# Second stage of a linear-attention and feed-forward kernel: VectorE's norms behind the quotients, ScalarE's copy of the transform's columns behind the upper part

## The reference

```python
qf, kf = elu(rope(x @ Wq.T)) + 1, elu(rope(x @ Wk.T)) + 1
num, den = causal_sums(qf, kf, v)            # per head and token
out = num / (den + 1e-6)
x = layernorm(x + out @ Wo.T)
h = fwht(x * SU_ug) / 64
h = silu(h @ W_gate.T * s_gate) * (h @ W_up.T * s_up)
h = fwht(h * SU_dp) / 64
x = layernorm(x + h @ W_down.T * s_down)
```

## Time and profile before

| | |
|---|---|
| time of the runs | 2311.16 us median of 3 (2309.01 to 2311.57) |
| span of the profiled execution | 2310.1 us (core 0, the only one); no time of its own is given beside it, so what lies around it is taken from the median of the runs, 1.1 us above |
| TensorE busy | 2254.4 us, 98% of the span |
| VectorE busy | 1825.1 us, 79% |
| ScalarE busy | 1273.1 us, 55% |
| GpSimd busy | 1129.0 us, 49% |
| DMA | 252.75 MB, 109 GB/s over the span |
| granted TensorE clock, mean | 0.994 |

### The profile page before, as it was taken

How to read it: one execution, slowest core, us unless ns; L and a number is a source line. 1 busy time by engine, 2 the same in 40 slices (tenths; PEclk the granted TensorE clock), 3 DMA queues, 4 the chain that set the end, 5 groups by cost and what they waited for, 6 DMA issues and landing times.

```text
span 2310.1 us, 32819 instructions
## 1 busy us (share of the span) xinstructions
PE 2254.4 (98%) x10209; PEld 1823.0 (79%) x10209; DVE 1825.1 (79%) x2452; ACT 1273.1 (55%) x2285; POOL 1129.0 (49%) x1002
## 2 busy tenths in 40 slices
PE   7999999999999999999999989999999999999998
PEld 5778787787878786787777768888888888888887
DVE  7877777778686868787887896787888788878877
ACT  6666666666676767233334455454545554455443
POOL 4667676767676767455544733321242133303321
PEclk9999999999999999999999999999999999999999
DMA  4110101111120215777767541323233323222323
GB/s 153 37 65 37 68 34 66 47 58 62 39 73 28 73 60 192 255 246 254 245 229 261 187 140 62 123 78 113 79 101 92 118 81 98 92 82 83 98 67 101
DMA packets 132701, 252.75 MB, mean 109 GB/s; under 512 B 44576, under 2 KB 45344, under 8 KB 122880
## 3 DMA queue, kind: packets, MB, share of 16 engines
q1 hardware_dynamic: 132608, 251.60, 32.5%
HBM read 188.11 MB, written 63.44 MB: 109 GB/s over the span
## 4 chain that ended last, share of the span: by engine, by line
PE 71%; issue 11%; POOL 9%; DVE 5%; ACT 2%; DMA 1%; SPq 0%; POOLq 0%; ACTq 0%; DVEq 0%
PE pj L548 17%; PE pj L629 11%; PE pnum L629 6%; PE pj L643 5%; PE psc L629 5%; PE pj L558 4%; PE pst L629 4%; PE psc L643 4%; PE pnum L643 3%; PE psc L579 3%; PE pnum L597 3%; PE pnum L600 3%; PE pst L643 2%; POOL fa L1338 2%; PE pst L586 1%
## 5 line engine op out<-in xcount | busy, mean ns | idle before, releaser
L1368 POOL TENSOR_TENSOR wcs<-wcr 128x256 f32<-128x256 f32 x64 | 67.7, 1058 | 515.3 <-DVE wcl L1107 504.3
L1401 POOL TENSOR_TENSOR tb<-tb,sinb 128x512 f32<-128x512 f32 x160 | 224.0, 1400 | 91.7 <-ACT tb L928 90.9
L548 PE MATMUL pj<-xah,wqh 128*128 128x512 f32 x512 | 204.3, 399 | 4.3 <-DVE Kf L1243 3.0
L1404 POOL TENSOR_TENSOR Ql<-tb,Qh 128x512 fp32r<-128x512 f32 x128 | 169.7, 1328 | 70.2 <-ACT Qh L937 70.1
L478 PE MATMUL pj<-woh,oh 128*128 128x512 f32 x512 | 202.9, 396 | 0.0
L548 PE MATMUL pj<-xal,wqh 128*128 128x512 f32 x512 | 200.5, 392 | 0.0
L548 PE MATMUL pj<-xah,wql 128*128 128x512 f32 x512 | 200.5, 392 | 0.0
L478 PE MATMUL pj<-woh,ol 128*128 128x512 f32 x512 | 200.4, 391 | 0.0
L478 PE MATMUL pj<-wol,oh 128*128 128x512 f32 x512 | 200.3, 391 | 0.0
L1231 DVE TENSOR_TENSOR pj<-pj,cosb 128x512 f32<-128x512 f32 x160 | 111.1, 694 | 69.7 <-ACT tb L928 69.6
L629 PE MATMUL pj<-xch,wch 128*128 128x512 f32 x384 | 150.9, 393 | 7.9 <-DVE xcl L1113 4.7
(11 more groups left out here) (258 smaller groups left out, 7070.8 us busy)
## 6 DMA issues: line engine op xcount, KB each, us to landing
num_scratch<-no SPq DMA_DIRECT2D x128, 256.0 KB, 2.4
nt<-num_scratch SPq DMA_DIRECT2D x32, 1024.0 KB, 5.5
rb<-rden_scratch SPq DMA_DIRECT2D x32, 1024.0 KB, 6.3
wdr<-wd_scratch SPq DMA_DIRECT2D x128, 256.0 KB, 3.3
wcr<-in_wg SPq DMA_DIRECT2D x64, 256.0 KB, 2.8
wcr<-in_wu SPq DMA_DIRECT2D x64, 256.0 KB, 3.1
xst<-in_xT SPq DMA_DIRECT2D x34, 256.0 KB, 3.8
xr<-in_x SPq DMA_DIRECT2D x32, 256.0 KB, 5.6
```

What stands on the lines that cost most here:

```text
L548: last = nc.tensor.matmul(bank[:, :], w[:, b, :], x[:, b, :], start=(k == 0), stop=(k == 11))
L1401: nc.gpsimd.tensor_tensor(tb[c][:, :], tb[c][:, :], sinb[:, :], ALU.mult).then_inc(sin_done, 1)
L1404: nc.gpsimd.tensor_tensor(Ql[g % 2][:, c, :], (tb[c] if c else Kf)[:, :], f32(Qh[g % 2][:, c, :]), ALU.subtract).then_inc(lo_done, 1)
```

## The change

On VectorE the quotient of block n+2 is put in front of the norm of block n-1, directly behind the lower part of block n+1; the order of a step becomes sums, lower, divide, norm, then columns_lo in j = 3. On ScalarE the copy `split(m-1)`, which rounds the transform's columns, leaves the end of step j = 2 and comes behind `upper` in step j = 3 of the same group. Nothing is added or removed, and no wait changes.

```diff
@@ ScalarE, step(m, j, at)
                 if at + 1 < NC:
                     upper(1 - s, n + 1, at + 1)
+                if j == 3 and at >= NCH:
+                    split(m - 1)
                 if at == 1:
@@
                 if j == 2 and at >= NCH:
                     fold_out(m - 1)
-                    split(m - 1)
                 if j == 3 and at >= NCH:
                     evict(m - 1)
@@ VectorE, step(m, j, at)
                 if at + 1 < NC:
                     lower(1 - s, n + 1)
+                if at + 2 < NC:
+                    divide(s, n + 2, m * 2 + j // 2 + 1)
                 if at >= 1:
                     norm(1 - s, n - 1)
                 if j == 3 and at >= NCH:
                     columns_lo(m - 1)
-                if at + 2 < NC:
-                    divide(s, n + 2, m * 2 + j // 2 + 1)
```

## The result

The changed kernel takes 2321.71 us (median of 5, 2319.49 to 2324.13), the kernel before 2311.16 us (median of 5): 10.6 us more, ratio 1.0048 with an interval of 1.0036 to 1.0060. It is slower, on the side that was forecast, and inside the full range of 2318 to 2338; it lies 0.3 us under the 2322 to 2332 of the forecast's own case, and the point, 2327.6, was 5.9 us too high.

A forecast was written before the change was run, and what follows sets the result against it. TensorE's matmuls bound the stage (busy 404.66 of 420 us), so only its waits count. Groups 14.1 plus opening 2.3 give 16.4 us; on the 2310.1 span, plus 1.1, 2327.6 us; range 2322 to 2332, with rivals 2318 to 2338.

The forecast's parts named there:

- the forecast's own case: Whole kernel: the worked-out sum of later norms holds, 2327.6 us, within 2322 to 2332; chance 0.71.
- j = 0, +1.86: First step of a group: quotient and GpSimd's scaling go before the norm, so TensorE's transposes start 1.86 us late.
- j = 1, +0.43: Second step of a group: quotient delays GpSimd's root, an addition precedes the norm; transposes wait 1.02 us, before 0.59.
- j = 2, -0.51: Third step of a group: the transposes no longer wait for the norm, where they waited 0.51 us before.
- j = 3, +0.27: Fourth step of a group: upper part goes before the copy, quotient before the norm; wait 0.4 us for 0.14.
- Opening, +2.3: Step 2 of the stage: a 2.3 us quotient lies before an already late norm, +2.3 us, bounds 0 to 4.
- The last group, +1.8: Last of seven groups: no quotient in j = 2 and 3, so it loses 1.8 us.
- Six groups, +12.3: The six groups before the last: each has the whole group sum of +2.05 us, +12.3 in all.
- A: VectorE's norm goes ahead of a waiting GpSimd instruction, saving 1.1 us in j = 0; 2320 us, chance 0.10.
- B: TensorE's granted clock falls in each of seven groups, 8.7 us on top; 2336 us, chance 0.10.
- C: Quotient fills VectorE's 2.94 us hole in j = 1 for nothing; -1.24 us a group, 2303 us, chance 0.04.
- D: Losses in j = 0 and gains in the rest cancel, added wait under 0.6 us; 2311 us, chance 0.05.

## Why the prediction was right, and where its sum was off

The forecast was slower by 16.4 us with 0.71 for its own case (2322 to 2332); it was slower by 10.6, 0.3 us under the foot of that case. The path that the forecast names is the one that the runs show; three of its terms were mis-sized, all of them too high. Its steps one by one:

- **j = 0, +1.86: measured +1.40.** The order quotient, scaling, norm is as worked out, and the scaling's turn was 0.96 us. The failed step is "the root waited during it and takes its turn of 0.3 to 0.4". The quotient at 1085.98 takes 2.28 us with the root still running to 1086.47 beside it: the root, one element a row, takes nothing from VectorE. That is 0.46 us a group, 2.8 in six groups; the other steps give 0.15 a group of it back.
- **j = 1, +0.43: measured +0.45.** Both causes, a root pushed back and an addition ahead of the norm, are in the rows. With the additions short the wait is 0, so all of it hangs on the additions; the two causes were not taken apart.
- **j = 2, -0.51: measured -0.51.**
- **j = 3, +0.27: measured +0.40.** The copy costs nothing where it stands; kept in front it would cost 1.8, and did (2.32 against 0.54).
- **Opening, +2.3: measured about 0** (974.47 - 974.95 = -0.5 at the transposes of step 3; the profiled execution of after comes to the stage's first matmul 0.8 us earlier). The failed step is "a quotient of 2.3 us now lies before that norm: +2.3". The quotient does lie there, but most of it falls into the 4.26 us for which VectorE waited for the root before, so the norm is 1.1 us later (962.45 for 961.31) and not 2.3. The first transposes waited 2.2 us, the second 1.3 instead of 3.2. Beside that, the kernel before loses clock behind its 3.05 us wait, and needs 13.04 us from these transposes to the next, where the changed kernel needs 11.43. In the changed kernel the clock fell one step earlier, where the loss lies in front of the next wait, and not there:

```profile
948.00:952.00 4.00, 3.28 (x12) 0.70 0.19 70
960.00:964.00 4.00, 2.83 (x16) 1.00 1.02 422
964.00:968.00 4.00, 4.00 (x19) 1.00 1.07 286
```

VectorE's rows there show also what the prediction priced too low: the quotient waits for its operands. The first row is the kernel before, the others are the changed one.

```profile
961.31 0.55 DVE L1005 TENSOR_SCALAR x<-x,mv,rstd 128x512 f32<-128x512 f32 x1 [4.26 <-POOL rstd L1321]
```

```profile
944.17 3.09 DVE L1034 TENSOR_TENSOR nt<-nt,rb 128x2048 f32<-128x2048 f32 x1 [1.97 <-DMA nt<-num_scratch]
...
960.24 2.29 DVE L1034 TENSOR_TENSOR nt<-nt,rb 128x2048 f32<-128x2048 f32 x1 [2.77 <-DMA rb<-rden_scratch]
```

- **The last group, +1.8: measured -1.2** (from the transposes of j = 3 before it, 1281.71 and 1271.83, to the last ones of the stage). The failed step is "the last has no quotient in j = 2 and 3 and loses 1.8": it takes j = 2 as in every group and says nothing of j = 3 and of the stage's end. Measured were waits of +1.28, +0.55, -0.88 and -0.51, and 1.6 us less where TensorE passes to the next stage.
- **Six groups, +12.3: measured +10.4** (307.24 for 296.88 us, from 974.47 and 974.95 to the same two places).

Opening, six groups and last group are too high by 2.8, 1.9 and 3.0 us; together that is 7.7, from the forecast's 16.4 to the 8.7 of the profiled pair. That the total still came out inside the range is owed to the six groups; opening and last group, forecast as losses, were none.

From the groups the profiled pair gives 2.6 + 5 x 1.74 - 2.5 = 8.8 us, against 8.7 read at the last transposes and 7.7 in the span; the medians differ by 10.6. The difference of up to 3 us between the pair and the medians lies within the 3.6 and 4.6 us by which runs of one kernel differ.

The rivals: A (the norm goes ahead of a waiting GpSimd instruction) did not happen, the norm of j = 0 takes 1.49 to 1.51 us in all seven groups. B (the clock, once a group) did not happen, the new waits being 1.4 us; it came at 2.2 us in the opening, where it cost nothing that shows, and at 2.3 us in groups of the kernel with the quotient alone. C (the hole is free) was tried by itself in the one step that has a hole and fell. D (losses and gains cancel) fell with the waits of 1.40 and 1.04 us.

Where the Trainium skill was weighed, the rows decided: the norm contends with GpSimd, 1.50 us against 0.54 in the changed kernel too. That does not go against the rule, which leaves out the two-port modes, and the norm's operation is on the section's list of those that can enter one; whether it does here no run shows. The same section's rule that the first to be issued keeps the port for its whole instruction ("SBUF — State Buffer", who interferes with whom) fits the rows shown here with GpSimd instructions of 512 elements; the root of j = 0, which ran to its end beside a quotient of undisturbed length (2.28 us), does not show the blocking that the rule has.

## What to carry to other kernels

An engine's idle time in front of a wait is not free room if the work put there holds something that the awaited engine needs. Here VectorE's hole was the time in which GpSimd's additions ran, and a quotient in it pushed the root, and so the norm, back (a wait of 2.6 us for 0.6); ask of each hole what the other engine does in it. Where a short instruction that many wait for stands in a queue behind long ones that nobody waits for yet, move the long ones (two additions moved by a step brought 8 us, from 4.0 to 12.2 under before) before touching the engine that waits. And put an instruction with a waiting consumer ahead of one whose consumer has slack: the quotient is needed a step later, the norm at once.

## What the runs showed that was not expected

- A GpSimd instruction on one element a row did not hold up VectorE's next instruction (the quotient behind the root, 2.28 us in j = 0 and in j = 2), while one on 512 elements does, by 0.96 to 1.1 us.
- The length of TensorE's wait alone does not say whether the granted clock falls from 2.4 to 1.2 GHz. With the quotient alone it fell at four of six waits of 2.3 us, and at none of the two in the opening, 2.2 and 3.2 us; with the quotient first in j = 1 at two of six of 2.6 us and not at 2.2 us in the opening, where the changed kernel's fell. No wait of the transposes of 1.8 us or less brought it down in any of the runs. A fall lengthened the group by 1.1 us (54.66 - 53.52) with the quotient alone and by 1.3 (52.20 - 50.86) with the quotient first in j = 1. Two stretches of TensorE of the kernel with the quotient first in j = 1, each around a wait of 2.6 us, the first with a fall and the second without:

```profile
1098.00:1102.00 4.00, 3.61 (x12) 0.58 0.68 215
1149.00:1153.00 4.00, 2.41 (x13) 1.00 0.43 122
```
- The same reordering costs 10.6 us in the kernel as it is and 17 us (2310.67 - 2293.74 = 16.9) with the additions short. Six groups cost about 11 us in either profiled pair. The difference lies at the ends: with the additions short the kernel before waits for nothing in the opening, and the reordered one is 7.0 us later behind it (986.59 - 979.62); in the kernel as it is the opening costs 0, with a wait that was there already, and the last group gives 2.5 back. A kernel that already waits can hide a new wait.
